# Linear attention in front of a mixture of experts: the attention's running state moved to small array tiles, its sum to SBUF

## The reference

```python
# causal linear attention, 16 heads of 16 features, chunks of 128 tokens
scores = where(mask, q_c @ k_c.T, 0)              # phi = elu + 1 on q and k
num = scores @ v_c + q_c @ S                      # S: 16x16 per head, running state
den = scores.sum(-1) + q_c @ z                    # z: the same with v = 1
S = S + k_c.T @ v_c;  z = z + k_c.sum(0)
y = num / (den + 1e-6);  out = y @ w_proj.T
# experts: top 1 of 8, 256 -> 1024 (relu) -> 256, with gate bias and expert bias
```

## Time and profile before

| | |
|---|---|
| median of 3 runs | 512.15 us (511.81 to 512.28) |
| span of the profiled execution | 510.7 us |
| execution's own time outside the span | not given by the page; the median lies 1.45 us above the span |
| TensorE busy | 489.6 us, 96% of the span |
| TensorE weight loads | 406.0 us, 79% |
| VectorE busy | 403.7 us, 79% |
| ScalarE, GpSimd busy | 280.9 us, 266.8 us |

### The profile page before, as it was taken

The page is one execution under the profiler, slowest core; times in us unless marked ns, Lnnn a source line. Parts: engine busy times, 40 slices in busy tenths (PEclk is TensorE's granted clock), DMA queues, the critical chain, the costliest instruction groups (busy, mean ns, idle before and its releaser), DMA issues.

```text
span 510.7 us, 17892 instructions
## 1 busy us (share of the span) xinstructions
PE 489.6 (96%) x6293; PEld 406.0 (79%) x6293; DVE 403.7 (79%) x881; ACT 280.9 (55%) x540; POOL 266.8 (52%) x465
## 2 busy tenths in 40 slices
PE   8699999999999999999998799999999999999996
PEld 8578887888878888788877688888888888888884
DVE  3798999999999999999889277766776776776775
ACT  3448887788877888877885033333332333333331
POOL 4345667767667676676663523344334344344222
PEclk9899999999999999999999799999999999999999
DMA  8525565565555655655442612122212212210000
GB/s 263 196 66 160 175 194 165 180 221 167 183 180 178 206 179 172 195 177 178 143 138 102 194 33 82 48 85 68 68 53 67 85 51 81 73 51 28 23 17 1
DMA packets 34306, 62.91 MB, mean 123 GB/s; under 512 B 5677, under 2 KB 10030, under 8 KB 34096
## 3 DMA queue, kind: packets, MB, share of 16 engines
q1 hardware_dynamic: 29232, 49.17, 30.1%
q0 software_dynamic: 4992, 12.60, 8.2%
HBM read 51.00 MB, written 13.50 MB: 126 GB/s over the span
## 4 chain that ended last, share of the span: by engine, by line
PE 82%; DVE 6%; POOL 5%; issue 4%; ACT 2%; DMA 1%; DVEq 0%; POOLq 0%; ACTq 0%
PE ps L654 21%; PE ps L667 20%; PE ps L401 7%; PE ps L443 6%; PE ps L472 5%; PE ps L516 5%; PE ps L456 4%; PE ps L486 4%; PE ps L419 3%; PE ps L502 2%; PE ps L623 2%; PE ps L426 1%; PE ps L508 1%; DVE AR L706 1%; PE ps L384 1%
## 5 line engine op out<-in xcount | busy, mean ns | idle before, releaser
L654 PEld LDWEIGHTS ps<-AR,W 128*128 x1872 | 132.2, 99 | 40.4 <-issue 1.5
L654 PE MATMUL ps<-AR,W 128*128 128x128 f16 x1872 | 156.9, 221 | 1.0 <-ACT AR L1227 0.9
L667 PE MATMUL ps<-W,ST 128*128 x624 | 150.5, 326 | 0.0
L1236 ACT ACTIVATE ST<-ST 128x512 f16<-128x512 f32 x78 | 49.2, 630 | 118.9 <-DVE ST L1056 118.9
L1056 DVE SCALAR_TENSOR_TENSOR ST<-ps,TAs,B1S 128x512 f32<-128x512 f32 x78 | 58.3, 748 | 52.7 <-PE ps L654 42.8
L1385 POOL DMA_INDIRECT out<-AR x39 | 39.7, 1017 | 109.2 <-DVE AR L1088 101.5
L1323 POOL TENSOR_TENSOR W<-ST,W 128x512 f16<-128x512 f32 x64 | 74.7, 1167 | 27.8 <-ACT W L1170 21.5
L762 DVE TENSOR_TENSOR AR<-ps,CT 128x512 f32<-128x512 f32 x128 | 81.9, 682 | 2.1 <-PE ps L443 2.1
L1068 DVE SCALAR_TENSOR_TENSOR ST<-ST 128x512 f16<-128x512 f32 x78 | 53.6, 687 | 15.6 <-ACT ST L1236 15.6
L1380 POOL DMA_INDIRECT AR<-scr,AR x39 | 48.7, 1250 | 30.6 <-DVE AR L1088 12.1
L401 PE MATMUL ps<-xT,WA 128*128 128x128 f16 x768 | 49.5, 222 | 3.7 <-ACT xT L1120 2.9
(11 more groups left out here) (147 smaller groups left out, 784.1 us busy)
## 6 DMA issues: line engine op xcount, KB each, us to landing
ST<-in_w SPq DMA_DIRECT2D x128, 256.0 KB, 4.1
scr<-XR SPq DMA_DIRECT2D x32, 256.0 KB, 2.1
XR<-in_x SPq DMA_DIRECT2D x32, 128.0 KB, 4.6
AR<-in_b SPq DMA_DIRECT2D x1, 1024.0 KB, 4.9
AR<-in_wall SPq DMA_DIRECT2D x2, 388.0 KB, 3.8
AR<-scr,AR POOLq DMA_INDIRECT x39, 3.7
out<-AR POOLq DMA_INDIRECT x39
ST<-in_cst SPq DMA_DIRECT2D x1, 576.0 KB, 4.4
```

Source lines behind the costliest of these rows:

```text
L654: a = e.matmul(dst, W[:, off:off + 57472][:, bass.ds(place_of(s), 128)], XT16[s % 2][:, xl * 256 + k * 128:xl * 256 + (k + 1) * 128], star ...
L667: a = e.matmul(PS[4 + s % 2][:, 0:w], src[h % 4][:, fs], W[:, off:off + 57344 + w][:, bass.ds(place_of(s), w)], start=(f == 0 and w == 512 ...
L1236: e.activation(HH[h % 4], H32[h % 2], ACT.Relu).then_inc(a_hh, 1)
```

## The change

- `inter` uses row tiles of 32 and column tiles of 64: per group g and row tile r one matmul of the 32 rows (2 heads) of T32 by the same rows of q, into bank 5 + r // 2, partitions 64 (r % 2) on. Banks 5 and 6 are now one tensor; a block of y.T stands in bank 5 + i at column 128 g. `pv`, `y1` and `yt1` follow that layout.
- `inter` stands directly behind `scores`.
- `st` uses column tiles of 32: per g and r one matmul of 32 columns of k by the 34 columns of its two heads of v, into 68 columns of bank 1 (beside `vg`'s output), without accumulation over chunks. It stands in front of `pv`, and one period earlier: `st(p - 2)`.
- `sm` on VectorE (in place of `t32`, behind masks 0 and 1) masks these 68 columns into SM; `state` on GpSimd adds SM to T32, or copies it for a batch's first chunk, between `xl` and the second `w_lo`.
- `vg(c)` waits for `sm(c-2)`, `vh(c)` for `st(c-1)`, `sm` for `lg`, `mx` and `place`, which share bank 1.
- In the drain, `inter(NC-1)` goes ahead of the warming matmuls, which write banks 1 and 0.

```diff
             for p in range(NC + 1):
                 if on(p - 3):
                     scores(p - 3)
-                    st(p - 3)
+                    inter(p - 3)
...
                 if on(p - 4):
                     yt1(p - 4)
-                if on(p - 3):
-                    inter(p - 3)
                 mxa(p)
...
+                if on(p - 2):
+                    st(p - 2)
                 if on(p - 3):
                     pv(p - 3)
...
# inter
-                    for i in range(2):
-                        j = 2 * g + i
-                        a = e.matmul(PS[5][:, j * 128:(j + 1) * 128], T32[:, g, 4 * i:4 * i + 4, :],
-                                     QK[c % 2][:, g * 128:(g + 1) * 128], start=(j == 0), stop=True,
+                    for r in range(4):
+                        rows, o = slice(32 * r, 32 * r + 32), 64 * (r % 2)
+                        a = e.matmul(PS[5 + r // 2][o:o + 64, g * 128:(g + 1) * 128], T32[rows, g, :, :],
+                                     QK[c % 2][rows, g * 128:(g + 1) * 128], start=(g == 0), stop=True,
                                      skip_group_check=True)
...
# st
-                    a = e.matmul(PS[6][:, g * 136:(g + 1) * 136], KT32[c % 2][:, g * 128:(g + 1) * 128],
-                                 V32[c % 2][:, 8 * g:8 * g + 8, 0:17], start=(c % CPB == 0 and g == 0),
-                                 stop=True, skip_group_check=True)
+                    for r in range(4):
+                        a = e.matmul(PST[32 * r:32 * r + 32, g * 34:(g + 1) * 34],
+                                     KT32[c % 2][:, g * 128 + 32 * r:g * 128 + 32 * r + 32],
+                                     V32[c % 2][:, 8 * g + 2 * r:8 * g + 2 * r + 2, 0:17], start=False,
+                                     stop=True, skip_group_check=True)
...
# VectorE
-                e.tensor_tensor(T32[:, :, :, 0:17], PS[6][:, 0:272].rearrange("p (g h e) -> p g h e", g=2, h=8),
-                                mh, ALU.mult).then_inc(S["t32"], 1)
+                e.wait_ge(S["lg"], c + 2)
+                e.wait_ge(t_mx, min((c + 3) // 4, E))
+                if c >= 10:
+                    e.wait_ge(t_rk, min((c - 10) // 8 + 1, 3))
+                if n_state(c) > 1:
+                    e.wait_ge(S["t32"], n_state(c) - 1)
+                e.tensor_tensor(SM, PST.rearrange("p (g a e) -> p g a e", g=2, a=2), ma, ALU.mult).then_inc(S["sm"], 1)
...
# ScalarE
-                e.activation(YT1, PS[5][:, :], ACT.Copy).then_inc(S["y1"], 1)
+                e.activation(YT1.rearrange("p (i n) -> p i n", i=2),
+                             PSS[5][:, :].rearrange("p (i n) -> p i n", i=2)[:, :, 0:256], ACT.Copy).then_inc(S["y1"], 1)
...
# GpSimd
+            def state(c):
+                if c % CPB == CPB - 1:
+                    return
+                e.wait_ge(S["sm"], n_state(c))
+                if n_inter(c) > 0:
+                    e.wait_ge(S["in"], n_inter(c))
+                if c % CPB == 0:
+                    e.tensor_copy(T32[:, :, :, 0:17], SM).then_inc(S["t32"], 1)
+                else:
+                    e.wait_ge(S["t32"], n_state(c) - 1)
+                    e.tensor_tensor(T32[:, :, :, 0:17], T32[:, :, :, 0:17], SM, ALU.add).then_inc(S["t32"], 1)
...
# the drain, TensorE
             scores(NC - 2)
-            st(NC - 2)
+            inter(NC - 2)
             yt1(NC - 3)
-            inter(NC - 2)
             yt2(NC - 3)
             pv(NC - 2)
             scores(NC - 1)
             pr(NC - 3)
-            e.wait_ge(S["t32"], n_state(NC - 2))
-            warm(30)
+            inter(NC - 1)
+            e.wait_ge(S["vh"], NC)
+            e.wait_ge(S["lg"], NC)
+            warm(30, PS[1][:, 0:128])
             yt1(NC - 2)
             place(3)
-            inter(NC - 1)
             pv(NC - 1)
             yt2(NC - 2)
             pr(NC - 2)
             yt1(NC - 1)
-            warm(24)
+            e.wait_ge(s_[0], NC)
+            warm(24, PS[0][:, 0:128])
```

More of the change, by code:

```diff
@@ L29 @@
 EXP = 255 << 23
-C_ID, C_MASK, C_ME, C_MH, C_ONE, C_WT, C_SL, C_PK, C_T, C_N = (
-    0, 128, 256, 258, 266, 274, 282, 282 + 5 * NP, 282 + 10 * NP, 283 + 10 * NP)
+C_ID, C_MASK, C_ME, C_ONE, C_WT, C_SL, C_PK, C_T, C_N = (
+    0, 128, 256, 258, 266, 274, 274 + 5 * NP, 274 + 10 * NP, 275 + 10 * NP)
 D_N = 72
@@ L76, in sem @@
             return ctx.enter_context(nc.semaphore(name))
-        PSS = {i: ctx.enter_context(nc.psum_tensor(f"ps{i}", [128, 1024 if i == 3 else 512], F32))
-               for i in (0, 1, 2, 3, 5, 6, 7)}
-        PS = [PSS[i][:, 0:512] if i != 4 else PSS[3][:, 512:1024] for i in range(8)]
+        PSS = {i: ctx.enter_context(nc.psum_tensor(f"ps{i}", [128, 1024 if i in (3, 5) else 512], F32))
+               for i in (0, 1, 2, 3, 5, 7)}
+        PS = [PSS[i - 1][:, 512:1024] if i in (4, 6) else PSS[i][:, 0:512] for i in range(8)]
         W = sb("W", [128, E * 8192], F16)
@@ L138, in program @@
         V32 = [ar(6912 + 512 * i, 512).rearrange("p (h e) -> p h e", h=16) for i in range(2)]
-        T32 = ar(7936, 512).rearrange("p (g h e) -> p g h e", g=2, h=8)
+        T32 = ar(7936, 128).rearrange("p (g a e) -> p g a e", g=2, a=2)
+        SM = ar(8064, 68).rearrange("p (g a e) -> p g a e", g=2, a=2)
         WPF = ar(8448, 512).rearrange("p (k n) -> p k n", k=2)
@@ L158, in py @@
             return PS[3] if c == NC - 1 else PS[2]
-        PMX = PS[1][0:2, 264:392]
-        PMA = PS[1][:, 392:394]
+        PST = PS[1][:, 264:332]
+        PMA = PS[1][:, 332:334]
+        PMX = PS[1][0:2, 336:464]
+        PRK = PS[1][:, 336:408].rearrange("p (e c) -> p e c", e=E)
         PBX = PS[7][0:8, 0:128]
@@ L166, in program @@
         msk = cc(C_MASK, 128).rearrange("p (o n) -> p o n", o=1).broadcast_to((128, 4, 128))
-        mh = cc(C_MH, 8).rearrange("p (o h z) -> p o h z", o=1, z=1).broadcast_to((128, 2, 8, 17))
+        ma = cc(C_ME, 2).rearrange("p (g a e) -> p g a e", g=1, e=1).broadcast_to((128, 2, 2, 17))
         par = cc(C_ME, 2).rearrange("p (g o n) -> p g o n", g=1, n=1).broadcast_to((128, 2, 2, 128))
@@ L193, in program @@
         RB8 = VA[:, 1776:1904].bitcast(BF16).rearrange("p (c e) -> p c e", e=E)
-        PRK = PS[1][:, 400:472].rearrange("p (e c) -> p e c", e=E)
         WAF = WA[:, :, :, :].rearrange("p l k n -> p (l k n)")
@@ L282, in program @@
         names = ("sums", "na", "nn", "nb", "xh", "xl", "xt", "xTc", "qk", "relu", "exp", "phi", "km", "sc", "pv", "ktr", "kt",
-                 "vg", "vh", "lg", "in", "st", "t32", "y1", "yt1", "y", "yt2", "y2", "pr", "res")
+                 "vg", "vh", "lg", "in", "st", "sm", "t32", "y1", "yt1", "y", "yt2", "y2", "pr", "res")
         S = {n: sem(f"s_{n}") for n in names}
@@ L358, in tensor, with warm @@
         def tensor(e):
-            def warm(n):
+            def warm(n, to=PS[6][:, 384:512]):
                 for _ in range(n):
-                    e.matmul(PS[6][:, 384:512], one16[:, :], one16[:, :], start=True, stop=True)
+                    e.matmul(to, one16[:, :], one16[:, :], start=True, stop=True)
             e.wait_ge(p_one16, 1)
@@ L410, in vg @@
                     e.wait_ge(S["vh"], c)
+                if c >= 2:
+                    e.wait_ge(S["sm"], n_state(c - 2))
                 if (c + 1) // 4 >= 1:
@@ L470, in pv @@
                             for o in range(2):
-                                j, b = 2 * g + i, 2 * t + o
-                                a = e.matmul(PS[5][32 * b:32 * b + 32, j * 128:(j + 1) * 128],
+                                b = 2 * t + o
+                                a = e.matmul(PS[5 + i][32 * b:32 * b + 32, g * 128:(g + 1) * 128],
                                              V32[c % 2][:, 8 * g + 4 * i + b, :],
                                              S32[2 * i + t][:, (2 * g + o) * 128:(2 * g + o + 1) * 128],
-                                             start=(c % CPB == 0 and j == 0), stop=True, skip_group_check=True)
+                                             start=(c % CPB == 0 and g == 0), stop=True, skip_group_check=True)
                 a.then_inc(S["pv"], 1)
@@ L482, in st @@
                 e.wait_ge(S["vh"], c + 1)
-                if n_state(c) > 1:
-                    e.wait_ge(S["t32"], n_state(c) - 1)
                 for g in range(2):
-                    a = e.matmul(PS[6][:, g * 136:(g + 1) * 136], KT32[c % 2][:, g * 128:(g + 1) * 128],
-                                 V32[c % 2][:, 8 * g:8 * g + 8, 0:17], start=(c % CPB == 0 and g == 0),
-                                 stop=True, skip_group_check=True)
+                    for r in range(4):
[3 more added lines that the diff above has]
+                                     stop=True, skip_group_check=True)
                 a.then_inc(S["st"], 1)
@@ L501, in yt1 @@
                 for j in range(4):
-                    a = e.transpose(py(c)[:, j * 128:(j + 1) * 128], YT1[:, j * 128:(j + 1) * 128], ID32)
+                    o = (2 * (j % 2) + j // 2) * 128
```

(18 more changed lines are left out.)

## The result

The changed kernel takes 514.32 us (median of 5 runs, 513.74 to 515.34) against 512.15 in the same comparison: ratio 1.0043, 95% interval 1.0031 to 1.0054. Forecast was 511.7 and no change. The span of the profiled executions went from 510.7 to 513.2 us; the changed kernel's was the longest of its five.

A forecast was written before the change was run, and what follows sets the result against it. It took `qk`'s wait for ScalarE's `xTc`, not TensorE's work, as the bound. Steady periods -0.5, fill +0.2, drain -0.2 us: sum -0.5, span 510.2; with 1.45 to the median, 511.7 us, range 507.3 to 518.5.

The forecast's parts named there:

- The main step: TensorE: `inter` covers ScalarE's `kt` and `xTc`; moved behind scores, it makes `qk` wait for `xTc` in every period.
- 7.88 for the ordinary period: Scores to next scores: 3.41 to `qk`, 4.27 from there, 0.20 for `st`; 7.88 us against 7.70.
- `inter` 0.60: TensorE, 32x64 tiles: 4 waves of 0.11 plus 0.16 for the switch, 0.60 us against 0.89.
- `st` 0.20: TensorE, ahead of `pv`: 16 records of 34 columns take 0.20 us, bounds 0.12 and 0.44, hidden by nothing.
- `state` 0.34: GpSimd, behind `xl`: the 68-column sum costs 0.34 us, bounds 0.22 and 1.16.
- the 0.2 for `sm`: Drain, bound by VectorE's queue: `sm` in place of `t32` gains 0.2 us.
- Without `inter` between, `mxa` can go at about 3.15: Periods with an expert's scale: `mxa` 3.15 after scores instead of 3.62, period 7.93 us, a gain of 0.29.
- p = 19: Period without `inter`: taken as 7.66 before, less about 0.07, plus 0.20 for `st`, 7.79 us.
- D: `st` on TensorE: short records' waves last as long as `pv`'s; +0.24 in 27 periods, +6.5, time 518.5; chance 0.18.
- 0.2 forecast for `st` in the fill: Ahead of the steady periods: two `st` are new, one of them on the chain, +0.2 us.
- B: Wait for `xTc` does not bind; TensorE's saving counts until GpSimd's `nn_begin` loop stops it: -4.5, time 507.6; chance 0.27.
- C: `inter` on TensorE: tiles of one bank go one after the other, 8 waves for 4, +0.44; +11, time 523; chance 0.10.

The follow-up runs named there:

- x7: Kernel before with only `inter`, still on the whole array, called directly behind scores: 524.50 us, ratio 1.0252.
- x1: Kernel before without `inter` and its waits, so the output lacks the state's part of y: 509.02 us, ratio 0.9928.
- x3: Changed kernel with `mx`, the transpose of the weights' maxima, ahead of `ktr` instead of behind `xt`: 513.71 us, 1.0012 of the kernel before.
- x10: Changed kernel with GpSimd's `state` ahead of `xl` and first weight split of even periods behind it, TensorE's order kept: 512.13 us, 0.9993 of the kernel before.
- x9: Kernel before with only GpSimd's first weight split of even periods moved behind `xl`: 510.17 us, ratio 0.9961.
- x2: Changed kernel with `inter` back between `yt1` and `mxa`, small tiles and new `st` kept: 512.99 us, 1.0001 of the kernel before.
- x4: Changed kernel with `inter` back between `yt1` and `mxa`, and GpSimd's `state` ahead of `xl`: 512.14 us, 0.9985 of the kernel before.
- x5: Changed kernel with `inter` behind `xt` and ahead of `yt1`: 511.82 us, 1.0010 of the kernel before.
- x6: Changed kernel with `inter` behind `xt`, ahead of `yt1`, and GpSimd's `state` ahead of `xl`: 509.58 us, 0.9966 of the kernel before.
- x8: Changed kernel with `inter` between `xt` and `yt1`, `state` ahead of `xl`, first weight split of even periods behind `xl`: 504.62 us, 0.9852 of the kernel before.
- x12: Kernel before with first weight split of even periods behind `xl` and whole-array `inter` between `xt` and `yt1`: 514.16 us, 1.0034.

## Why the prediction was wrong

**Right, with sizes.** The main step, that `inter` covers `kt` and `xTc` and stalls `qk` from its new place, holds (chain of p = 15, x7, x1): forecast 7.88 for the ordinary period, measured 7.87 in eight of nine and 7.99 in one. `inter` 0.60 forecast, 0.60 measured. `st` 0.20 forecast, 0.27 in the chain (0.24 between the starts of `st` and `pv`); the 0.04 to 0.07 too little was offset by scores to `qk` at 3.35 instead of 3.41, where the switch back to the whole array cost `ktr` 0.16 instead of 0.20. That 7.88 was met so closely is in part luck. `state` 0.34 forecast, 0.31 measured; `sm` 0.22 busy. The stretch behind the steady periods gained nothing, as forecast for `inter`; the 0.2 for `sm` did not come.

**Wrong: the periods with an expert's scale.** The failed step is "Without `inter` between, `mxa` can go at about 3.15". I wrote that its wait, VectorE's `largest`, would be over then, from a queue of masks, `sm` and `largest`. I put down nothing for the transposes `mx`, although the same text moved all that stands behind scores 0.14 later and named `mx` among `sm`'s new waits, as "for work done about 1 us before". It is done just as VectorE comes to `sm`. VectorE's timeline, ordinary period (first two rows) and the one with a scale:

```profile
120.01 1.29 DVE L768 TENSOR_TENSOR AR<-ps,CT 128x512 f32<-128x512 f32 x2
121.22 0.22 DVE L781 TENSOR_TENSOR AR<-ps,CT 128x68 f32<-128x68 f32 x1
...
127.89 1.29 DVE L768 TENSOR_TENSOR AR<-ps,CT 128x512 f32<-128x512 f32 x2
129.31 0.23 DVE L781 TENSOR_TENSOR AR<-ps,CT 128x68 f32<-128x68 f32 x1
```

`sm` starts 1.21 behind the start of the masks in the one and 1.42 in the other, where `mx` ends at 129.13. That brings `mxa` to 3.35 by records, `qk` to 3.66 where 3.46 was forecast, and the period to 8.19 instead of 7.93. The eight periods lost 2.4 us against their forecast, which is over nine tenths of the 2.6 by which the whole steady part missed (-0.42 forecast by kind, +2.13 measured). x3 took that wait away and got 1.8 of the 2.4 back in those periods, 1.6 us in the total. Another 0.3 is in periods 10, 11, 18, 19, 26 and 27: they grew by 1.06 where 0.75 was forecast, and x10 and x9 show that the loop over GpSimd and VectorE is what holds them.

The 3.15 itself came from two errors that cancelled. "3.0 after scores" subtracts a start by the chain from an end by records; alike it is 128.25 - 125.17 = 3.08. And VectorE's masks now begin 1.21 after scores instead of 1.36. With the wait for `mx` gone, x3 has `mxa` at 3.13 in seven of the eight periods.

Three smaller sums are off and change nothing. With p = 19 at 7.59 before, its forecast should have been 7.72 instead of 7.79 (measured 7.83, and 7.68 in p = 11). The terms for D, 6.5 and 5.4 us, lead from 511.7 to 518.2 and 517.1, not to 518.5 and 517.5.

**In the fill: the clock.** In the profiled execution of the changed kernel TensorE's granted clock fell to the lower level (0.5 in the profile, 1.2 GHz) about 2 us earlier than in that of the kernel before. Windows from 18 to 20 us, first of the kernel before, then of the changed one (TensorE busy first, clock third from the end):

```profile
18.00:20.00 2.00, 0.98 (x8) 0.77 (x8) 0.94 (x3) 1.01 (x4) 1.75 (x6) 1.00 0.86 281
```
```profile
18.00:20.00 2.00, 1.51 (x8) 1.26 (x8) 0.86 (x3) 0.56 (x4) 1.75 (x6) 0.54 0.79 249
```

In both TensorE had stood idle from about 15.6 to 18.5 us. Scores of the first chunk began at 25.01 instead of 23.92; 0.7 of the 1.1 us was absorbed by the next period. x2 and x4 fell to half clock about as late as before, x3 as early as the changed kernel. This is not shown to be an effect of the change: x5 and x6 have the same instructions up to there and differ in the same way (clock 0.57 and 1.00 from 18 to 20 us), and the mean clock of the changed kernel's five executions goes from 0.985 to 0.993. Why the fall comes where it does is open. With the fall as late as before, x2 and x4 have scores of p = 4 at 30.78 and 30.76 by records, against 30.62 before; that is near the 0.2 forecast for `st` in the fill.

**The rivals.** B was not the case in most periods, but its loop holds the six named above and is the next bound: x6 and x8 show it. C falls: 16 records took 0.60 with two row tiles on each bank in different halves of its partitions, so they did not go one after the other. Of the two pages of the Trainium skill that the prediction sets side by side, the rule by groups of partitions of "PSUM — Partial Sum Buffer" fits this trace, though its section on bank collisions gives it for two engines and repeats there the ban for row tiles. D falls at its full size: 0.27 for 16 short records with their start, not 0.44. But the 0.24 from which the prediction let D decide was reached; the earlier `qk` made up for it. By the floor that the Trainium skill gives ("TensorE: Matmul & The Clock Gate", section Back-to-back issue gap) the estimate for `st` was 0.40; in tiles the trace has 0.24 to 0.27, so the measurement decides against applying it there.

The range held the time; the chances (0.36 for slower against 0.34) said little. With the periods with a scale at their measured length the steady sum would have been +1.9 in place of -0.5, and the forecast would have been slower.

## What to carry to other kernels

Busy time on the engine that fills the chain is not the price of its instructions: look for the one period of the loop in which the instruction is missing, and compare the two lengths; here 0.89 us of work was worth 0.11 where it stood (p = 19), and 0.15 at most in an ordinary period (x1). Take both starts from the same view: the chain and the records differ by about 0.07, enough to turn 0.11 into 0.04. When a block moves within an in-order queue, list every semaphore behind it, and for each reader its new margin in numbers; an estimated "about 1 us before" has to be computed once everything ahead of it has moved. A block made shorter should stand where an engine waits for two others at once: `inter` behind `xt` filled the waits for VectorE's mask and for ScalarE's evictions together, and then the loop over GpSimd was the next bound and needed an edit of its own.

## What the runs showed of the hardware

- Sixteen float32 records of 34 columns on four column tiles take 0.24 us by starts, ahead of records in the same mode: 15 ns each. `pv`'s 128-column records take 32 ns each there.
- Going back from 32x64 tiles to the whole array showed as 0.38 for the two transposes of `ktr` against 0.22 in periods without a switch ahead of them (x7's and before's chains).
- A float32 tensor_scalar of VectorE from SBUF to SBUF that met a 512-column tensor_tensor of GpSimd lasted until that was over: in x6 eight `nb` took 0.70 to 1.22 instead of 0.40 and each ended 0.15 after the split; in x12 a 2-column one took 0.78 instead of 0.22 and ended 0.02 after `km`.
- In the periods with a scale a semaphore that came just as VectorE's queue reached its instruction cost about 0.2 us: `mx` ended at 129.13, the masks ahead of `sm` at 129.18, and `sm` began at 129.31 instead of 0.08 before the masks' end. In x3, with `mx` over at 128.34, it began 1.21 behind the masks' start again (127.60, 128.81).
